# First group's norm moved into the edge stage's last places, and second products three slices behind the first

## What is computed

```
x = x + gnn(layernorm(x))
    q, k, v = x@Wq + bq, x@Wk + bk, x@Wv + bv            # 4 heads of 64
    alpha   = sum(q[dst] * k[src]) / sqrt(64)            # 53125 edges, sorted by dst
    a       = softmax of alpha over the edges of one dst
    out     = segment_sum(a * v[src], dst) + x@Wskip + bskip
    h       = layernorm(x + out) * g1 + be1
    x_new   = layernorm(h + gelu(h@W1 + b1)@W2 + b2) * g2 + be2
x = x + experts(layernorm(x))
    w = softmax(mean(x)@Wr + br)                         # 8 experts
    sum over e of w_e * (relu(bn(relu(bn(x@W1_e + b1_e))@W2_e + b2_e))@Wo_e + bo_e)
```

## Time and profile before

| | us |
|---|---|
| median of 3 runs | 1477.23 |
| the profiled execution, its own time | 1477.81 |
| its span, first to last instruction | 1476.0 |
| PE busy in the span | 1238.7 (84%) |
| DVE busy | 1069.5 (72%) |
| POOL busy | 917.5 (62%) |
| ACT busy | 800.7 (54%) |
| mean granted TensorE clock | 0.94 |

### The profile page before, as it was taken

One profiled execution on the slowest core, in us unless ns is written; L12 is line 12 of the kernel. 1 busy time (PEld: TensorE's weight loads), 2 busy tenths in 40 slices (PEclk: granted clock), 3 DMA queues, 4 the chain that ended last, 5 costly groups with the idle time before them and its releaser, 6 DMA issues. The chain is left out here.

```text
span 1476.0 us, 24097 instructions
## 1 busy us (share of the span) xinstructions
PE 1238.7 (84%) x6835; PEld 955.4 (65%) x6835; DVE 1069.5 (72%) x2557; ACT 800.7 (54%) x2505; POOL 917.5 (62%) x883
## 2 busy tenths in 40 slices
PE   7989677777677677767677889999999999999999
PEld 3444454455445444544455578889798899999998
DVE  7747877887777777878787789886757656555655
ACT  1255857575757575766667555555543344444443
POOL 3265666666666666666564556866766477667765
PEclk9998988888998998899888999999999999999999
DMA  7476766666766676667665120111000000000002
GB/s 224 154 237 199 238 193 200 184 199 183 200 189 201 184 201 187 197 181 203 181 199 142 33 75 29 46 34 37 13 15 22 1 22 15 9 21 15 1 12 77
DMA packets 74071, 175.39 MB, mean 119 GB/s; under 512 B 11500, under 2 KB 36651, under 8 KB 73945
## 3 DMA queue, kind: packets, MB, share of 16 engines
q0 software_dynamic: 37632, 124.28, 30.1%
q1 hardware_dynamic: 34641, 48.25, 9.8%
q10 hardware_dynamic: 1672, 1.33, 0.3%
HBM read 159.91 MB, written 13.91 MB: 118 GB/s over the span
## 5 line engine op out<-in xcount | busy, mean ns | idle before, releaser
L687 POOL DMA_INDIRECT ring<-kv_rows,k_srcI x464 | 459.5, 990 | 284.2 <-issue 122.4
L757 ACT ACTIVATE ring<-ring 128x64 f32<-128x64 f32 x1800 | 438.9, 336 | 11.9 <-issue 10.8
L1290 POOL TENSOR_TENSOR wm<-k_gf,wm 128x512 fp32r<-128x512 f32 (+2 forms) x224 | 258.9, 1159 | 144.1 <-DVE wm L1791 144.1
L1389 ACT ACTIVATE k_gf<-psF,k_scT 128x512 f32<-128x512 f32 (+2 forms) x224 | 162.0, 724 | 252.2 <-PE psF L1560 248.9
L807 PE MATMUL psA<-ring,oh 128*128 128x260 f32 x912 | 273.7, 429 | 10.4 <-DVE k_acc L1016 8.0
L777 PE MATMUL psQ<-k_q,ohT 128*128 x1392 | 225.1, 302 | 60.0 <-issue 53.4
L1791 DVE CAST wm<-k_gf 128x512 fp32r<-128x512 f32 (+2 forms) x224 | 159.5, 719 | 155.7 <-ACT k_gf L1389 155.7
L982 DVE TENSOR_TENSOR prod<-psQ,ring 128x512 f32<-128x512 f32 x232 | 157.6, 679 | 82.7 <-remote 33.1
L777 PEld LDWEIGHTS psQ<-k_q,ohT 128*128 128x128 bf16 x1392 | 129.7, 104 | 118.5 <-issue 87.1
L807 PEld LDWEIGHTS psA<-ring,oh 128*128 128x128 f32 x912 | 177.6, 216 | 38.5 <-ACT ring L757 9.2
L1022 DVE TENSOR_REDUCE alpha<-prod 128x8 f32<-128x512 f32 x232 | 155.7, 671 | 0.2
(11 more groups left out here) (283 smaller groups left out, 2644.9 us busy)
## 6 DMA issues: line engine op xcount, KB each, us to landing
ohT<-step_destinations SPq DMA_DIRECT2D x29, 512.0 KB
ring<-kv_rows,k_srcI POOLq DMA_INDIRECT x464
kv_rows<-kvst SPq DMA_DIRECT2D x25, 260.0 KB, 2.4
we<-in_L_ffn_W SPq DMA_DIRECT2D x16, 256.0 KB, 2.8
residual<-qst SPq DMA_DIRECT2D x25, 128.0 KB
xs<-in_x SPq DMA_DIRECT2D x2, 1024.0 KB, 9.0
resin<-residual SPq DMA_DIRECT2D x4, 512.0 KB
we<-in_L_ffn_Wo SPq DMA_DIRECT2D x8, 256.0 KB, 2.8
```

The source lines that it names most:

```text
L687: nc.gpsimd.indirect_dma_start(out=ring[:, LT * (j % CP) + k, j // CP:j // CP + 2, :].rearrange("p t e -> p (t e)"), out_offset=None, in_= ...
L757: last = nc.scalar.activation(row[:, 0:D], row[:, 0:D], ACT.Copy, scale=row[:, D:HW_])
L1290: nc.gpsimd.tensor_tensor(low[:, i % 2, m, 0:w], gf[:, n % 4, 0:w], high[:, i % 2, m, 0:w], ALU.subtract).then_inc(s_gl, 1)
L1389: nc.scalar.activation(gf[:, n % 4, 0:cols(g)], ps, ACT.Relu, bias=bias, scale=scale).then_inc(s_ev, 1)
```

## The change

Two things. First, DVE's work on the first group of the tail (3 blocks: denominators, values, norm) goes into the edge stage, at places 232 to 237 and 246, as `first_group(n)` with n = place - 232, each piece behind what DVE does in that place anyway. Its rows lie in `qst` (`y0`), and its root on POOL stands behind POOL's last one-hot matrices. In the tail, DVE begins with the split of W1; ACT splits W1's quarters 0 and 2, then copies the first group's columns, then splits 1 and 3; PE transposes at once, with one dummy product behind each half in place of seven ahead (`keep_busy`). Second, `S_LAG` is 3 in place of 2. The diff, with declarations, semaphore names and a moved wait left out:

```diff
--- before.py
+++ after.py
@@ -62,7 +62,7 @@
 CH = [3, 4, 4, 4, 4, 3, 3]
 NC = len(CH)
 NPT = NC * FC
-S_LAG = 2
+S_LAG = 3
 NE = 8
 XP = [(0, 4), (4, 12), (12, 20), (20, NB)]
 EV = TP // 16 * 16
@@ -579,6 +579,12 @@
         fx = sb("fx", [1, H])
         fac = sb("fac", [BP, H])
         qst = sb("qst", [BP, 2, 2 * HID])
+        y0 = qst[:, :, :].rearrange("p a (b d) -> p (a b) d", d=HID)[:, 0:CH[0], :]
+        res0 = wqs[:, :, :].rearrange("p k (t d) -> p (k t) d", d=HID)[:, 0:CH[0], :]
+        den0 = sb("den0", [BP, CH[0], H])
+        st0 = sb("st0", [BP, CH[0], 6])
+        mv0 = sb("mv0", [BP, CH[0], 2])
+        ve0, rs0, mh0 = [sb(n, [BP, CH[0]]) for n in ("ve0", "rs0", "mh0")]
 
         psQ = [pb(f"psQ{b}", [P, 512]) for b in range(NQ)]
         psA = [pb(f"psA{b}", [P, 512]) for b in range(NA)]
@@ -603,6 +609,9 @@
         s_reso = [sem(f"s_reso{b}") for b in range(2)]
         s_w1, s_row, s_hvd, s_res = sem("t_w1"), sem("t_row"), sem("t_hvd"), sem("t_res")
         keep.update(s_w1=s_w1, s_row=s_row, s_hvd=s_hvd, s_res=s_res)
...
+        keep.update(s_den=s_den, s_y=s_y, s_yr=s_yr, s_st1=s_st1, s_c1=s_c1, s_h=s_h, s_mv0=s_mv0, s_ve0=s_ve0, s_rs0=s_rs0)
         res_v = io["res"].rearrange("(t p) d -> p t d", p=BP)
 
         drel_row = io["drel"].rearrange("s l -> (s l)")
@@ -690,6 +699,7 @@
                         in_offset=bass.IndirectOffsetOnAxis(ap=keep["srcI"][:, LT * step + k:LT * step + k + 1], axis=0)
                     ).then_inc(s_kv[j % CP], 16)
 
+            nc.gpsimd.memset(mh0[:, :], -0.5).then_inc(s_half0, 1)
             walk(at)
             for b in range(LATE, STEPS):
                 if b < STEPS - NO:
@@ -700,6 +710,9 @@
                     last = nc.gpsimd.tensor_scalar(onehot(b, k), iotaF[:, 0:BP], dstR[:, LT * b + k:LT * b + k + 1],
                                                    None, ALU.is_equal)
                 last.then_inc(s_ohp, 1)
+            pool.wait_ge(s_half0, 1)
+            pool.wait_ge(s_ve0, 1)
+            nc.gpsimd.tensor_tensor(rs0[:, :], ve0[:, :], mh0[:, :], ALU.pow).then_inc(s_rs0, 1)
 
         @block.scalar
         def _(act):
@@ -966,6 +979,53 @@
                     nc.vector.tensor_scalar(fac[:, :], psM[0:BP, 400:400 + H], noh[:, at_noh:at_noh + 1], None,
                                             ALU.add).then_inc(s_mv, 1)
 
+            def first_group(n):
+
+
+                if n == 0:
+                    ends = acc[:, 0:CH[0], :].rearrange("p t (h e) -> p t h e", h=H)[:, :, :, D]
+                    nc.vector.tensor_scalar(den0[:, :, :], ends, 1e-16, None, ALU.add).then_inc(s_den, 1)
+                    dve.wait_ge(s_den, 1)
+                    nc.vector.reciprocal(den0[:, :, :], den0[:, :, :]).then_inc(s_den, 1)
+                if n == 1:
+                    dve.wait_ge(s_den, 2)
+                    for b in range(2):
+                        dve.wait_ge(s_reso[b], 16 * len(range(b, NB, 2)))
+                    nc.vector.tensor_tensor(
+                        y0.rearrange("p t (h d) -> p (t h) d", h=H),
+                        acc[:, 0:CH[0], :].rearrange("p t (h e) -> p (t h) e", h=H)[:, :, 0:D],
+                        den0[:, :, :].rearrange("p t h -> p (t h)").unsqueeze(2).broadcast_to([BP, CH[0] * H, D]),
+                        ALU.mult).then_inc(s_y, 1)
+                if n == 2:
+                    dve.wait_ge(s_res, 16)
+                    dve.wait_ge(s_y, 1)
+                    nc.vector.tensor_tensor(y0, y0, res0, ALU.add).then_inc(s_yr, 1)
+                if n == 3:
+                    dve.wait_ge(s_yr, 1)
+                    for u in range(CH[0]):
+                        last = nc.vector.bn_stats(st0[:, u, :], y0[:, u, :])
+                    last.then_inc(s_st1, 1)
+                if n == 4:
+                    dve.wait_ge(s_st1, 1)
+                    for u in range(CH[0]):
+                        last = nc.vector.bn_aggr(mv0[:, u, :], st0[:, u, :])
+                    last.then_inc(s_mv0, 1)
+                    dve.wait_ge(s_mv0, 1)
+                    nc.vector.tensor_scalar(ve0[:, :], mv0[:, :, 1], LN_EPS, None, ALU.add).then_inc(s_ve0, 1)
+                if n == 5:
+                    dve.wait_ge(s_row, 64)
+                    for u in range(CH[0]):
+                        last = nc.vector.scalar_tensor_tensor(out=y0[:, u, :], in0=y0[:, u, :], scalar=mv0[:, u, 0:1],
+                                                              in1=keep["g1b"][:, :], op0=ALU.subtract, op1=ALU.mult)
+                    last.then_inc(s_c1, 1)
+                if n == SUM_LAG - 2:
+                    dve.wait_ge(s_c1, 1)
+                    dve.wait_ge(s_rs0, 1)
+                    for u in range(CH[0]):
+                        last = nc.vector.scalar_tensor_tensor(out=acc[:, u, 0:HID], in0=y0[:, u, :], scalar=rs0[:, u:u + 1],
+                                                              in1=keep["be1"][:, :], op0=ALU.mult, op1=ALU.add)
+                    last.then_inc(s_h, 1)
+
             def at(i, j, fresh):
                 step = RING * i + j
                 cc, q, jj = CR * i + j // CP, j // CP, j % CP
@@ -1038,6 +1098,8 @@
                         dve.wait_ge(s_acc, br)
                     row = acc[:, bass.ds(blk, 1), :].rearrange("p a (h e) -> p (a h) e", h=H)
                     nc.vector.tensor_tensor(row, row, fac[:, :].unsqueeze(2).broadcast_to([BP, H, HW_]), ALU.mult).then_inc(s_resc, 1)
+                if step >= STEPS:
+                    first_group(step - STEPS)
 
             walk(at)
 
...
@@ -1297,10 +1359,9 @@
                                         ALU.subtract).then_inc(s_wl, 1)
 
             nc.gpsimd.memset(mh[:, :], -0.5).then_inc(s_half, 1)
-            pool.wait_ge(s_half, 1)
-            root(0, 0)
             for k in range(KC):
                 columns("T", 0, k)
+            pool.wait_ge(s_half, 1)
 
             for p in range(NPT):
                 g, m = p // FC, p % FC
@@ -1401,10 +1462,12 @@
                 nc.scalar.activation(w1h[:, q // 2, (q % 2) * CW:(q % 2 + 1) * CW], gf[:, q, :], ACT.Copy).then_inc(s_wh, 1)
 
             act.wait_ge(s_w1, 16)
-            for q in (0, 2, 1, 3):
+            for q in (0, 2):
                 w1_high(q)
             for k in range(KC):
                 columns("T", 0, k)
+            for q in (1, 3):
+                w1_high(q)
             for q in range(4):
                 act.wait_ge(s_we[q], 16)
                 nc.scalar.activation(w2h[:, 2 * q:2 * q + 2, :], we[:, q, :].rearrange("p (m n) -> p m n", m=2), ACT.Copy).then_inc(s_wh, 1)
@@ -1599,9 +1662,9 @@
                     nc.tensor.matmul(psF[3][:, :].rearrange("p (a n) -> p a n", a=4), ident[:, :],
                                      iotaF[:, :].unsqueeze(1).broadcast_to([P, 4, P]), start=True, stop=True)
 
-            keep_busy(7)
             for k in range(KC):
                 columns("T", 0, k)
+                keep_busy(1)
             bank_free(("b1",))
             pe.wait_ge(s_row, 64)
             nc.tensor.transpose(psT[:, 0:FC], b1r[:, :], ident[0:FC, 0:FC]).then_inc(s_pt, 1)
@@ -1665,7 +1728,7 @@
                     ALU.mult).then_inc(s_y, 1)
                 dve.wait_ge(s_res, 16 * g + 16)
                 dve.wait_ge(s_y, g + 1)
-                nc.vector.tensor_tensor(y[:, 0:n, :], y[:, 0:n, :], (res0 if g == 0 else res)[:, 0:n, :], ALU.add).then_inc(s_yr, 1)
+                nc.vector.tensor_tensor(y[:, 0:n, :], y[:, 0:n, :], res[:, 0:n, :], ALU.add).then_inc(s_yr, 1)
                 dve.wait_ge(s_yr, g + 1)
                 for u in range(n):
                     last = nc.vector.bn_stats(st[:, 0, u, :], y[:, u, :])
...
@@ -1833,9 +1894,6 @@
                 nc.vector.reciprocal(rec[:, a:b, :], rec[:, a:b, :]).then_inc(s_den, 1)
                 dve.wait_ge(s_den, done + 2)
 
-            denominators(0, CH[0], 0)
-            values(0)
-            normed(0)
             for a, q in enumerate((0, 2, 1, 3)):
                 at = slice(q % 2 * CW, (q % 2 + 1) * CW)
                 dve.wait_ge(s_wh, a + 1)
```

More of the change, by code:

```diff
@@ L605, in attend @@
         keep.update(s_w1=s_w1, s_row=s_row, s_hvd=s_hvd, s_res=s_res)
+        s_den, s_y, s_yr, s_st1, s_c1, s_h = [sem("t_" + n) for n in ("den", "y", "yr", "st1", "c1", "h")]
+        s_mv0, s_ve0, s_rs0, s_half0 = sem("t_mv0"), sem("t_ve0"), sem("t_rs0"), sem("t_half0")
+        keep.update(s_den=s_den, s_y=s_y, s_yr=s_yr, s_st1=s_st1, s_c1=s_c1, s_h=s_h, s_mv0=s_mv0, s_ve0=s_ve0, s_rs0=s_rs0)
         res_v = io["res"].rearrange("(t p) d -> p t d", p=BP)
@@ L1082, in tail @@
         tmp = sb("tmp", [NP, 2, P])
-        res0 = keep["wqs"][:, :, :].rearrange("p k (t d) -> p (k t) d", d=HID)
         b1c = sb("b1c", [P, FC])
@@ L1116, in tail @@
         s_half, s_gl, s_tl, s_wl, s_nm = [sem("t_" + n) for n in ("half", "gl", "tl", "wl", "nm")]
-        s_ve = [sem(f"t_ve{k}") for k in range(3)]
-        s_rs = [sem(f"t_rs{k}") for k in range(3)]
```

(9 more changed lines are left out.)

## The result

| | before | changed |
|---|---|---|
| median, us (4 runs each, same chip) | 1476.84 (1475.62 to 1482.57) | 1487.11 (1485.95 to 1487.73) |
| profiled execution, us | 1477.81 | 1486.7 |
| its span, us; granted clock of PE | 1476.0; 0.940 | 1484.9; 0.932 |
| waits of DVE for PE ahead of the sums (`summed`) of the feed-forward stage's groups | 6.1 us in 2 | 22.9 us in 6 |

The ratio is 1.0046, 95% interval [1.0024, 1.0068]: slower, by some 6.8 us. The forecast was 1478.3 within 1472.5 and 1486.0. The measured median lies 1.1 us above that range; the forecast's own mark, 1477.23, times the ratio gives 1484.0, inside it.

What follows compares the result with a forecast made beforehand. The prediction took the dense layer's loop through DVE, ACT, POOL and PE as the tail's bound, with DVE late. Edge stage +5.4 less tail 4.3 gave +1.1 us: 1478.3 against a median of 1477.23, range 1472.5 to 1486.

Steps and rivals of the forecast that it cites:

- Edge stage, +5.4 forecast: Edge stage's last places: moved DVE work delays `dif` 3.85, last piece adds 1.0, POOL 0.6; 5.4 us, bounds 2.5 and 12.
- the six pieces: Reciprocal, values, residual add, statistics, aggregate and variance, subtraction: moved DVE operations ahead of `dif`, 5.20 us in bare durations.
- The 0.6 for POOL's interference: Edge stage's last places: POOL's comparisons may delay DVE's residual add and three operations at place 237; 0.6 us taken.
- Tail until T(1,0), 5.4 us sooner forecast: Start of the tail: the loop starts 5.4 us earlier, estimated between DVE's 4.9 and PE's 7.2.
- The expected wait of PE for normed(1): Ahead of group 1's transposes in the tail: a new PE wait of some 3.5 us for DVE's normed(1).
- The third slice brings nothing there: Dense layer's loop: nothing waits for a second product, so no gain there; one more second product at the end, 1.06 us.
- tail -4.3: Whole tail: 5.4 us gained less 1.06 for the last second product, 4.3 us faster, bounds 2 and 8.2.
- The first (places absorb more): Rival, edge stage: last places absorb more than counted; edge 2.5, tail -5.4, sum -2.9, 1474.3 us; chance 0.20.
- The second (POOL in the last places): Rival, edge stage: POOL holds off DVE at places 234 and 237; +4.7, 1481.9 us, or 1485; chance 0.15.
- The third (the new wait costs the clock): Rival, ahead of group 1's transposes: PE's 3.5 us wait halves its clock; 1.5 to 2 us more, 1480; chance 0.13.
- The fourth: Rival, tail's start: first group isn't ready because its root comes last; within 1 us of the forecast; no chance given.
- The third sign: Dense layer in the changed profile: the loop from one shift to the next again takes 28.9 us.

Runs made afterwards that it cites:

- dummies: `move_only` with one dummy product of 512 columns on PE at each of places 233 to 239; 1352.19 us, ratio 1.0026 against the kernel before.
- lag3_only: The kernel before with S_LAG = 3 and nothing else changed; 1485.65 us, ratio 1.0035 against the kernel before.
- lag3_rest: The kernel before with second products two slices behind in the first group, three from slice 8 on; 1352.07 us, ratio 1.0024.
- lag3_warm: The kernel before with S_LAG = 3 and three dummy 512-column products on PE ahead of group 1's first transposes; 1351.72 us, ratio 1.0016.
- lag3_again: `lag3_only` once more, on another chip, beside `lag3_warm`; 1354.45 us, ratio 1.0036 against the kernel before.
- move_only: The changed kernel with S_LAG back at 2, so only the first group's norm moved; 1482.17 us, ratio 1.0010 against the kernel before.
- late_pieces: `move_only` with the first group's pieces all behind `dif` instead of ahead of it; 1480.53 us, ratio 0.9996 against the kernel before.
- last_hot: `late_pieces` with the last step's one-hot matrix built by DVE instead of POOL; 1347.49 us, ratio 0.9985; repeated at 1349.21 us, 0.9993.

## Why the forecast was wrong

**Edge stage, +5.4 forecast: measured +5.59** at PE's first instruction, right in its mechanism and in part by luck in its number. Within it, `dif` was to be 3.85 late and is 4.37, with all durations at about their bare size: that is the 5.20 of the six pieces less the two waits of 0.85, and the 0.5 that I counted as covered at place 237 was not. The 0.6 for POOL's interference did not come (1.33 us for the three operations). From `dif` to the last addition I gave 1.0; it is 13.79 - 11.68 = 2.1. PE's stretch there, in the changed kernel:

```profile
832.84 0.27 PE L846 MATMUL psM<-k_ident,Gm 64*128 64x64 f32 x1 [0.86 <-DVE Gm L970]
...
835.79 7.60 PE L820 MATMUL psA<-ring,oh 128*128 128x260 f32 x20 [0.87 <-DVE k_acc L1076]
```

```profile
834.00:840.00 6.00, 4.95 (x14) 3.66 (x13) 3.90 (x12) 5.45 (x23) 3.36 (x6) 0.58 0.00 0
```

The other 1.0 us is PE at the slower clock, by `dummies`. So the last addition is 6.48 us late against 5.45 in the forecast. Of that 0.9 came back at the hand-over (2.55 in place of 3.44 us from the last addition to POOL's first instruction of the tail), of which the forecast said that it stays; it follows POOL's last instruction, below.

**Tail until T(1,0), 5.4 us sooner forecast: half right, measured 3.4.** Counted from the tail's first instruction, values(1) came after 11.6 us (forecast 11.4), the first product after 7.5 (forecast 6). The expected wait of PE for normed(1) was there, 4.50 for 3.5. The other 2 us: I let normed(1) follow values(1) in the 9.30 us of before. It took 862.21 to 873.53, 11.32, because the same instructions, now sooner, met POOL at work: residual add 1.83 in place of 1.22, last piece 4.50 in place of 3.08. POOL in the changed kernel:

```profile
862.70 3.55 POOL L1344 TENSOR_TENSOR gT<-k_gf,gT 128x384 fp32r<-128x384 f32 x2 [7.20 <-ACT gT L1439]
...
868.65 4.60 POOL L1344 TENSOR_TENSOR gT<-k_gf,gT 128x384 fp32r<-128x384 f32 x4
```

Before, POOL's pair took 2.49 us and began 0.56 us behind the residual add; now it began 0.83 us ahead of it. Between POOL's later ones were gaps before, and now there are none. The rule of the Trainium skill that the forecast weighed ("SBUF — State Buffer", who interferes with whom) has two-input operations of DVE and POOL's reads exclude each other. Both stretches fit it, but the side that pays differs: in the tail DVE too, 1.83 for 1.22 and 4.50 for 3.08; in the edge stage POOL alone, 2.47 and 1.85 for 1.18, while DVE's pieces kept their bare durations.

**"The third slice brings nothing there; `summed` comes one slice later, inside DVE's wait for the router": this step failed.** Its ground, that nothing waits for a second product, was read from the steady groups of before, where DVE comes to the sum later than PE. For the first group it is false: the trace of before has a wait of 3.57 us at 882.08. The slice was to cost 1.06 us and costs some 5.2 (`lag3_only`). What it does:
- It puts one more slice's first product ahead of the first sum, while PE is the late one: 1.4 us (`lag3_rest`, 13.54 for 12.18 from T(1,0) to `summed(0)`). A second product of 1.06 us, which stood ahead of T(1,0), stands behind it too, and a wait of 0.58 us that PE had there before (876.83) is filled: in all 1.9 us (`lag3_warm` against before, clock at 1.00 in both).
- It empties PE ahead of T(1,0). I had this wait, priced it at nothing because DVE would be late anyway, and kept its clock for a rival. But the engine that is late behind the wait is PE, so up to the first sum both the wait and the 1.4 to 1.8 us of slower clock count.
- In later groups the sum comes after DVE needs it: six waits, 20.1 us in the traces of `lag3_only` and `lag3_again`, against two, 6.1. From the norm of piece 1 to that of piece 5 these kernels lose no more than those with two slices, so this is slack as the forecast had it.
- At the end it costs 1.07 us, as forecast.

**Sum.** Forecast +1.1: edge +5.4, tail -4.3. Measured to the experts +7.28: edge +5.59; to T(1,0) -3.42; to `summed(0)` +4.28; from there to the norm of piece 1 -1.85, as DVE used part of its wait to work ahead; from there to piece 5 +1.60, where `move_only` has +1.32; from piece 5 to the experts +1.08, the last second product (1.06 forecast).

**Rivals.** The first (places absorb more) is wrong: `dif` 4.37 late. The second (POOL in the last places) is wrong in its place and right in another. The third (the new wait costs the clock) is what happened, at about the price that I gave it, 1.5 to 2 us, as far as the first sum (its comparison takes DVE's 3.47 us of the hand-over; PE's own wait was 4.04), but it had 0.13 and was not joined with the order's own cost. The fourth can't be: the first group was ready when the tail began (847.09, and 850.66).

**Signs.** `dif` came as late as forecast, and PE had its wait (4.50 for 2 to 4). The third sign, a loop of 28.9 us, was not met, 29.88 between the norms of pieces 1 and 2, but it says nothing of the third slice: `move_only` has 29.90.

## What to carry to other kernels

Before calling a reordering free "because engine A is the late one", look up A's own waits in each stretch that it touches, the first round of a loop above all: a wait of A for B at one place there says that B is late at that place, whatever holds in the steady rounds. In this kernel a deeper lag between producer and consumer products filled one wait and was paid where a sum was due that something waited for, in the first group, and once more at the end of the chain; in the groups between it cost nothing. Work that is put into gaps of a chain belongs behind the chain's last link, not ahead of it, if it isn't itself needed by then (`late_pieces` against `move_only`: 4.6 us sooner `dif`, 4.0 us sooner tail; in time, 0.9996 against 1.0010, the two are not told apart).

## What the runs showed of the hardware

- PE ran at 1.2 GHz behind waits of 4.50 us (from the first instruction on) and 2.59 us (from 0.4 us on in `lag3_only`, from 1.2 us on in `lag3_again`), and also in the last places of the edge stage, where it had only waits under 1 us in a row (0.86, 0.18, 0.87) between short work. Filling either kept it at 2.4 GHz there, and a drop then fell elsewhere: 1 us won at one place was lost at another in `dummies` and `lag3_warm`. The same code has its stretches at half clock in other places in another execution: `lag3_only` 212 to 216 us behind the last `alm` and none at 184 to 190, `lag3_again`, on another chip, the other way about. So a trace's position within 2 us, far behind an edit, says little.
- The hand-over between the two stages follows POOL's last instruction. In 12 of the 14 traces POOL's first instruction of the tail starts 5.55 us behind its last one of the edge stage, with PE's interval anywhere from 2.0 to 4.5 us and ACT's from 6.8 to 8.6. Where POOL was done 1.4 us earlier (the two of `last_hot`) its interval grew to 6.03 and PE's fell to 0.98. The two rows of the changed kernel:

```profile
844.18 0.89 POOL L715 TENSOR_TENSOR rs<-ve,mh 128x3 f32<-128x3 f32 x1
850.62 0.10 POOL L1361 MEMSET mh<- 128x4 f32 x1 [5.55 <-POOLq L539]
```

- The same kernel took 1480 us on one chip and 1350 on two others. From the last `alm` to the experts it is the same length (220.85 and 220.58 in `lag3_only` and `lag3_again`); all of the difference is in the edge stage, which ran 134 us shorter. The first 400 us, `before` on the first kind of chip, then `lag3_again` (the same code there) on the other:

```profile
0.00:400.00 400.00, 308.93 (x1388) 184.94 (x1388) 296.36 (x809) 229.62 (x852) 227.33 (x243) 0.91 0.68 202
```

```profile
0.00:400.00 400.00, 329.31 (x1669) 203.58 (x1669) 352.85 (x968) 278.38 (x1063) 269.42 (x284) 0.99 0.78 233
```

Transfers ran at 233 GB/s in place of 202 and the clock at 0.99 in place of 0.91. Which of the two is the cause, these runs don't tell. Kernels are compared only with runs of before on their own chip.
